# A one-core attention and feed-forward kernel: context, energy and projection products of the middle batches as three f32r products of high and low parts, in a new order of all engines

## What is computed

```python
# attention over features, ctx: (4, 512, 256), Wq, Wk: (128, 256)
query  = einsum('bnc,dc->bnd', ctx, Wq) + bq
key    = einsum('bnc,dc->bnd', ctx, Wk) + bk
attn   = softmax(einsum('bnd,bmd->bnm', query, key), axis=-1)
x      = x + einsum('bln,bmn->blm', layernorm(x), attn)
# feed-forward; gate_w, up_w (2048, 512), down_w (512, 2048) are splines of 8,134 control points each
h      = layernorm(x)
inter  = silu(einsum('bsh,ih->bsi', h, gate_w)) * einsum('bsh,ih->bsi', h, up_w)
x      = x + einsum('bsi,hi->bsh', inter, down_w)
```

## Time and profile before

| | us |
|---|---|
| median of 3 runs | 296.62 (294.58 to 297.31) |
| the profiled execution | 297.34 |
| its span, first to last instruction | 295.4 |
| TensorE busy in the span | 278.2 |
| VectorE, ScalarE, GpSimd busy | 179.8, 153.9, 157.8 |
| start of the three turns and of the last batch (`project`) | 66.1, 127.4, 188.7, 250.1 |

### The profile page before, as it was taken

One profiled execution on the slowest core, in us unless ns is written; L12 is line 12 of the kernel. 1 busy time (PEld: TensorE's weight loads), 2 busy tenths in 40 slices (PEclk: granted clock), 3 DMA queues, 4 the chain that ended last, 5 costly groups with the idle time before them and its releaser, 6 DMA issues.

```text
span 295.4 us, 4068 instructions
## 1 busy us (share of the span) xinstructions
PE 278.2 (94%) x1298; PEld 199.5 (68%) x1300; DVE 179.8 (61%) x318; ACT 153.9 (52%) x259; POOL 157.8 (53%) x139
## 2 busy tenths in 40 slices
PE   8699489899999999999999999999999999799995
PEld 3132157654777888946868888657688888477894
DVE  1697988985466676743467856524677577343403
ACT  3044733224888923256899422458897132376710
POOL 5589252778565772225855723058547521598630
PEclk9958869999999999999999999999999999999999
DMA  7997044000900000036200000333000001100003
GB/s 204 376 426 290 0 124 163 0 2 0 354 3 0 3 0 2 21 121 237 118 0 0 0 0 0 142 118 166 0 0 0 0 0 71 71 0 3 0 0 144
DMA packets 7212, 23.34 MB, mean 79 GB/s; under 512 B 1185, under 2 KB 2337, under 8 KB 5793
## 3 DMA queue, kind: packets, MB, share of 16 engines
q1 hardware_dynamic: 7200, 23.20, 21.1%
HBM read 19.01 MB, written 4.19 MB: 79 GB/s over the span
## 4 chain that ended last, share of the span: by engine, by line
PE 81%; DVE 10%; DMA 2%; ACT 2%; POOL 2%; issue 1%; SPq 1%; DVEq 0%; POOLq 0%
PE bank L1287 11%; PE bank L1289 10%; PE bank L1318 10%; PE bank L1150 6%; PE bank L1304 5%; PE bank L1273 5%; PE bank L1301 5%; PE bank L1302 5%; PE bank L1325 4%; PE bank L1247 4%; PE bank L1248 4%; PE bank L1249 4%; PE bank L1161 3%; PE bank L1204 3%; DVE prod L872 2%; DMA power<-in_g_power 2%
## 5 line engine op out<-in xcount | busy, mean ns | idle before, releaser
L1108 POOL TENSOR_TENSOR il<-inter,ih 128x512 fp32r<-128x512 f32 x64 | 86.6, 1366 | 46.3 <-ACT ih L788 29.4
L958 DVE TENSOR_TENSOR inter<-inter,bank 128x512 f32<-128x512 f32 x64 | 43.6, 685 | 45.6 <-ACT inter L784 45.5
L784 ACT ACTIVATE inter<-bank 128x512 f32<-128x512 f32 x64 | 37.9, 596 | 17.0 <-PE bank L1289 14.4
L788 ACT ACTIVATE ih<-inter 128x512 fp32r<-128x512 f32 x64 | 39.3, 629 | 2.4 <-DVE inter L958 2.3
L759 ACT ACTIVATE qk<-bank,nmr,rstd 128x512 f32<-128x512 f32 x16 | 12.5, 779 | 40.0 <-PE bank L1249 22.5
L1318 PEld LDWEIGHTS bank<-d_r,ih 128*128 128x128 f32 x256 | 30.8, 191 | 2.1 <-ACT ih L788 1.0
L1318 PE MATMUL bank<-d_r,ih 128*128 128x192 f32 x256 | 31.1, 274 | 0.0
L1287 PE MATMUL bank<-xh,gate_r 128*128 128x512 f32 x64 | 27.3, 426 | 1.5 <-DVE zg L950 1.5
L1301 PE MATMUL bank<-ih,d_u 128*128 128x512 f32 x64 | 28.0, 437 | 0.0
L1096 POOL TENSOR_TENSOR xres<-x,ones 128x2048 f32<-128x2048 f32 x4 | 14.4, 3600 | 23.9 <-DMA out<-xres 23.6
L1287 PE MATMUL bank<-xh,up_r 128*128 128x512 f32 x64 | 25.6, 400 | 0.0
(11 more groups left out here) (97 smaller groups left out, 519.3 us busy)
## 6 DMA issues: line engine op xcount, KB each, us to landing
...
knots<-in_d_knot SPq DMA_DIRECT2D x1, 1280.0 KB, 11.6
...
```

Source lines behind the costliest of these rows:

```text
L784: nc.scalar.activation(inter[:, m % 3], gbank[m % 2][:], ACT.Silu).then_inc(s["silu_done"], 1)
L788: nc.scalar.activation(ih[:, m], inter[:, m % 3], ACT.Copy).then_inc(s["ih_done"], 1)
L958: V.tensor_tensor(inter[:, m % 3], inter[:, m % 3], ubank[m % 2][:], ALU.mult).then_inc(s["mult_done"], 1)
L1108: G.tensor_tensor(il[:, m % 2], inter[:, m % 3], ih[:, m].bitcast(f32), ALU.subtract).then_inc(s["il_done"], 1)
```

## The change

**Products.** `project` of every batch, and `qk` and `energy` of batches 1 to 3, are made of three f32r products in place of one fp32: high x high, low x high, high x low. Batch 0's context and energy remain fp32 (`first(b)`).

**Parts.** Three new stages make them: `split_basis` (ScalarE rounds 408 columns, VectorE subtracts) and `split_weights` (512 columns) in the preparation, `split_ctx` (1024 columns) at the head of each turn, into the room of xl. `qk` leaves its low parts by a VectorE pass each (`qk_l`). `cast_t` now takes xn2r (ScalarE, high) and xn2l (VectorE, low) from PSUM; the fp32 copy `xn2T` is gone, and xn2l uses pl's room. The bank of a transpose is free only after VectorE's pass.

TensorE's `keep_warm` 10 stands behind the energies of batch 0 and 11 to 19 up to the last `prob_t`; before, 10 to 14 stood around `prob_t` and `xm`, and 15 to 19 between spreads 11 and 12. The diff, cut to its core:

```diff
+        wqk_h, wqk_l = (sb(f"wqk_{n}", [P, 2, CTX // P, DK], f32r) for n in "hl")
+        qk_h, qk_l = (sb(f"qk_{n}", [P, 2, TOK], f32r) for n in "hl")
+        ctx_h, ctx_l = xl[:, 0:2], xl[:, 2:4]
...
             load(win[:, 0, 0:HID // 2], "g_node", "gwin_in")
+            load(masks[:], "ident", "ident_in")
+            load(pick[:].rearrange("p k n -> p (k n)"), "g_pick", "pick_in")
+            load(power[:], "g_power", "power_in")
+            load(coef[:], "g_coef", "coef_in")
+            load(g_basis[:].rearrange("p a n -> p (a n)"), "g_basis", "basis_in")
+            load(r2g[:], "g_r2", "r_in")
+            load(r3g[:], "g_r3", "r_in")
+            load(bqk[:, 0:1], "bq", "bqk_in")
             load(win[:, 1, 0:HID // 2], "u_node", "uwin_in")
             load(win[:, 1, HID // 2:HID], "u_win", "uwin_in")
+            sp.dma_start(x[:], d["x"][0]).then_inc(s["x_in"], 16)
+            sp.dma_start(ctxT[:], d["ctxT"][0]).then_inc(s["ctx_in"], 16)
...
-                    sp.wait_ge(s["qk_mm"], 2 * b + 4)
+                    sp.wait_ge(s["ctx_split"], b + 1)
...
+                def split_ctx(b):
+                    act.wait_ge(s["ctx_in"], 16 * (b + 1))
+                    act.wait_ge(s["xm_mm"], NT * b)
+                    nc.scalar.activation(ctx_h, ctxT[:], ACT.Copy).then_inc(s["ctx_hi"], 1)
...
-                    nc.scalar.activation(xn2T[:, t], abank[t % 2][:], ACT.Copy).then_inc(s["xn2t_copied"], 1)
+                    nc.scalar.activation(xn2r[:, t], abank[t % 2][:], ACT.Copy).then_inc(s["xn2r_done"], 1)
...
+                        V.scalar_tensor_tensor(qk_l[:, n], abank[n][:], bqk[:, n:n + 1], qk_h[:, n].bitcast(f32), ALU.add, ALU.subtract).then_inc(s["qkl_done"], 1)
...
+                def split_ctx(b):
+                    dve.wait_ge(s["ctx_hi"], b)
+                    V.tensor_tensor(ctx_l, ctxT[:], ctx_h.bitcast(f32), ALU.subtract).then_inc(s["ctx_split"], 1)
...
-                    V.tensor_copy(xn2r[:, t], xn2T[:, t]).then_inc(s["xn2r_done"], 1)
+                    V.tensor_tensor(xn2l[:, t], abank[t % 2][:], xn2r[:, t].bitcast(f32), ALU.subtract).then_inc(s["xn2l_done"], 1)
...
+                        pe.wait_ge(s["wqk_split"], 1)
+                        pe.wait_ge(s["ctx_split"], b)
+                        pe.wait_ge(s["xn2l_done"], NT * b)
...
+                                mm(abank[n][:], wqk_h[:, n, c], ctx_h[:, c], start=start, stop=False)
+                                mm(abank[n][:], wqk_l[:, n, c], ctx_h[:, c], start=False, stop=False)
+                                last = mm(abank[n][:], wqk_h[:, n, c], ctx_l[:, c], start=False, stop=stop)
...
-                        pe.wait_ge(s["xn2t_copied"], NT * b + t - 1)
+                        pe.wait_ge(s["xn2l_done"], NT * b + t - 1)
...
-                    pe.wait_ge(s["xn2t_copied"], NT * (b + 1))
+                    pe.wait_ge(s["xn2r_done"], NT * (b + 1))
...
-                        last = mm(zgbank[0:G_K, :], g_basis[:, a], xn2T[:, a], start=a == 0, stop=a == CLS - 1)
+                        mm(zgbank[0:G_K, :], g_basis_h[:, a], xn2r[:, a], start=a == 0, stop=False)
+                        mm(zgbank[0:G_K, :], g_basis_l[:, a], xn2r[:, a], start=False, stop=False)
+                    for a in range(CLS):
+                        pe.wait_ge(s["xn2l_done"], NT * b + a + 1)
+                        last = mm(zgbank[0:G_K, :], g_basis_h[:, a], xn2l[:, a], start=False, stop=a == CLS - 1)
```

411 lines of the change are left out of this document (227 added, 184 removed).

## The result

| | before | changed |
|---|---|---|
| median time, us | 296.89 (294.58 to 297.31) | 301.54 (301.18 to 302.40) |
| ratio | 1 | 1.0186 [1.0151, 1.0220] |
| profiled execution: span (whole run) | 295.4 (297.34) | 299.5 (301.63) |
| first gate tile | 73.0 | 77.8 |
| turns 1 and 2, from `project` to `project` | 61.32, 61.36 | 61.04, 61.06 |

The ratio is the recorded one, with its interval, from four runs of each kernel; the quotient of the two medians alone is 1.016. The forecast was 296.4 and "within 1%", with a range of 291 to 299.9; the kernel became slower by 1.9% (by 4.65 us on the medians) and lies above that range. Both halves of the sum missed, to the same side: in the traces the preparation lost 4.75 us where 2.3 were forecast, and everything behind the first gate tile gained 0.7 where 2.5 were forecast.

What follows compares the result with a forecast made beforehand. TensorE was taken to bound the turns and VectorE the preparation. Profiled span 295.4 - 2.5 (loop and end) + 2.3 (preparation) = 295.2, on the median 296.4 us; range 291 to 299.9.

Steps and rivals of the forecast that it cites:

- Both halves of the sum: Preparation to the first gate tile loses 2.3 us; the loop and the end gain 2.5 us.
- Three products at 0.69: On TensorE, three f32r products cost 0.69 us against 0.86 for one fp32 product, saving 0.17 us per product.
- The stall before the context product: At a turn's edge, `qk` waits for VectorE's low part of the context; 0.7 us lost.
- The stall behind gate tile 15: Inside a turn, TensorE's last three products of `down` 0 wait about 0.55 us for ScalarE's round 15.
- Half clock when `project` starts: At the preparation's end, TensorE without fillers runs products at 0.44 instead of 0.23 us; total preparation loss 2.3, otherwise 1.4.
- Rival C: Three products cost what fp32 costs, so nothing is saved; 299.9 us. Chance 0.05, shared with a missed wait in the turn.
- rival B's mechanism: Half clock over both `project` and `qk` of the first turn, low past 77 us; 299.9 us, chance 0.13.
- the term for 10.6 to 38.3 us: In the preparation, VectorE's work from the first residual through residual 7 takes 27.7 us without a gap.
- the gain of a turn: Each turn of the loop gains 0.85 us, not the 2.0 us of work removed from TensorE.
- The edge: From the end of xm 3 to the first gate tile takes 14.67 us instead of 15.21, a gain of 0.55.
- The middle: From the first gate tile to the end of xm 3, a net gain of 0.3 us.
- the last edge: At the edge into the last batch, 0.68 us saved in `project` less 0.2 gives a gain of 0.5.

Runs made afterwards that it cites:

- e3: Changed kernel with project, qk and energy of the middle batches as one fp32 product of high parts each, low parts made but unused; ratio 1.0338.
- e7: Kernel before in its old orders and transfers, all splits of the change made, but each product one fp32 product of the high parts; ratio 1.0248.
- e5: Kernel before with only the energies of batches 1 to 3 made as three f32r products; ratio 0.9943.
- e6: Kernel before in its old orders and transfers, with energies and projection as three products and the context product fp32; ratio 1.0020.
- e4: Products and splits of the change, with all lists (preparation, loop, loads) of the kernel before; ratio 1.0113.
- e12: Kernel before with `split_weights` put behind residual 11 and `split_basis` behind residual 12, results not used; ratio 1.0127.
- e17: e4 with TensorE's spreads 14 and 15 put ahead of transposes 2 and 3 of the preparation; ratio 1.0214.

## Why the prediction was wrong, point by point

**Right.** Three products at 0.69 against 0.86 (measured: 0.68, and e3 and e7 price the difference at 1.1 to 1.2 us a turn). The stall before the context product (0.7 forecast, 0.62), released by VectorE's low part behind a table load. The stall behind gate tile 15, by ScalarE's round 15 (0.55 forecast, 0.22). Half clock when `project` starts (0.50 over 64 to 72 us), and cheaper than forecast: from the low part of the context to the first gate tile 3.26 us instead of 2.76, so 0.5, not 0.9. Rival C is out by e3, rival B's mechanism too: the clock was back at 74.

**The preparation: the term for 10.6 to 38.3 us was mis-sized.** "27.7 us, to 38.3, no gap that I find." It took 31.3, and started 1.0 later. The prediction priced each VectorE pass as if its inputs were ready and GpSimd left it alone; the trace shows three things in that stretch:
- the first residual at 11.6 instead of 10.6: its second factor landed 1.0 us behind VectorE's readiness;
- window split 1 at 1.31 instead of 0.66 (priced as a node pass; alone it lasts 0.75), the split of x at 2.90 instead of 2.3: both work between SBUF tiles and stood behind a pass of GpSimd (rows above);
- gaps of 2.0 us, for ScalarE's half of the node weights (0.9), the context product (0.7) and the energy (0.4), and 0.4 us in small ones. TensorE, whose granted clock is 0.58 over 14 to 24 us, feeds all three; the prediction counted VectorE's work there and took TensorE as ready. That it is the clock that makes them late was not tried, and the kernel before has such gaps too, 2.1 us on its node weights.

Behind it 0.45 and 1.3 us came back: `down_factors` took 1.4 us, not the 2.64 of the earlier trace rows, one of whose four passes had stood beside GpSimd's mults (1.51 us long, the others 0.40 to 0.55). Sum: 1.0 + 3.6 - 0.45 - 1.3 = 2.9 late at the last residual, less 0.4 at the clock: 2.5, which is 77.8 against 75.3. (The prediction's own terms behind the last normalisation add up to 70.55, not 70.45.)

**The timed runs lose more than the trace shows:** 6.2 us before the first gate tile, where the traces have 4.75; the traced run of the kernel before was one of its slower ones (297.34, median 296.89). By the ladder of kernels, each step with a noise of 1 to 2 us: energies 0 (e5, -0.4), basis split and casts from PSUM 2.0 to 2.4 (e6), weights and context on top 2.3 (e4), list and transfers 1.9 (the changed kernel against e4). The passes added last 1.4 us in e6 (basis 0.58, casts 4 x 0.2) and cost 2.0; 3.3 us in e4 (with 0.68 and 1.22) and cost 4.3; 1.25 us in e12, right in front of `project`, and cost 3.7. The prediction took them at their durations, or covered. e12 shows one way (the clock), e4 and e17 a second (transposes that wait for low parts, and a spread behind them), and passes that stand behind GpSimd are a third. How much of the 6.2 each has in an average execution is not settled; the single traces differ by 1 to 2 us there.

**The loop: the gain of a turn was 0.29, not 0.85.**
- The edge gave 0.15 instead of 0.55. From the end of xm 3 to T 8.56 instead of 8.46, and from T to the first gate tile 6.51 instead of 6.2: ctx_h 1.06 and ctx_l 1.23 against 0.98 and 1.15, which I had scaled from passes of twice the columns as if they had no fixed part, 0.06 between engines at each step, and products 0.01 slower each. No wait is listed ahead of the first transposes, where 0.25 was forecast (its terms, 4.41 less 4.24, give 0.17). The waits of transposes 2 and 3 were seen in the prediction, their size was not: e6 shows that the transposes' wait for low parts gives back all that `project` saves (0.62 for 0.63).
- The middle gave 0.14 instead of 0.3. Energies are worth 0.45 in the old order (e5); the new order behind tile 15 lost 0.3 of it (45.98 against 45.66 in e4).
- At the last edge `project` and what follows to the first gate tile took 0.61 less (0.68 forecast), and from the end of xm 3 to `project` 0.29 more (0.2 forecast). From the last `project` to the end of the span only 0.30 of the 0.61 is left; why, no run tells.

**The chances.** Slower had 0.18, and only by the clock, the product rate or an unseen wait. What spoke for more was in the rows: VectorE at 51.86 of 58.40 us was the bound of the preparation, and the change puts its passes exactly there, once, to save work on TensorE that repeats three times. The forecast priced passes at their duration in the one stretch where an engine has no slack.
